# An audio tower on one core: sparsemax refinement over eight rows at once, and expert gathers one expert further ahead

## Chip, core and metric

The kernel runs on one core of a Trainium2 chip. The metric is the device time of one launch in microseconds (us), smaller is better. It was run three times, and one further execution was recorded by the hardware profiler.

## What is computed

The reference has three parts, cut here to what matters:

```python
h = tokens(x)                                  # patches of 200 samples, rfft, |.| and angle, 202->808 gelu ->128
# attention with sparsemax, 16 sequences of 256 tokens, 8 heads of 64
sim  = einsum(q, k) * 64**-0.5                 # 256x256 scores per head
attn = maximum(sim - tau, 0)                   # tau per row: the row of attn sums to 1
h = h + (attn @ v) @ W_out + b_out
# experts: each of 8 experts takes the 1024 tokens of highest probability (softmax over all 4096 tokens)
vals, idx = top_k(softmax(xn2 @ Wr, axis=0).T, 1024)
out_e = gelu(xn2[idx] @ W1 + b1) @ W2 + b2
h = h + zeros.at[idx].add(vals * out_e)
```

## The kernel before

The 4096 tokens are 32 tiles of 128, in 8 groups of 512 tokens (two sequences each). Three stages follow one another.

**Front and attention rounds.** Spectra and token features come first. Then each round handles the attention of one group, while TensorE (PE) also does the token layers and the q, k, v projections of later groups. The order on PE and ScalarE (ACT) is the list `PLAN` (L66), the order on VectorE (DVE) is `STEPS` (L85). Both are written by hand, and semaphores join them. A group's scores are four pairs `d` (0 to 3) of score tiles; a pair has two halves `u` of four rows of 128x256, so eight rows per partition. For each pair DVE takes the largest 8 of every row (`largest`, L1038), the next 8 (`thresholds` L1050, or `laced_thresholds` L1074), computes a threshold `tau` from these 16, and compares the sixteenth with `tau` (L1068, L1099). If it is above, more than 16 values may count and the threshold may need refinement. Two small reductions (L1070 and L1071) say this for each half and for both; GpSimd (POOL) takes the maximum over partitions (`anymore`, L453, L457). `settle` (L1184) reads the result into a register and branches. Where a half is marked, `surplus` (L1108) sums `max(score - tau, 0)` for its four rows (L1111) and tests whether any sum exceeds 1 by more than 3e-6; if so, `newton` (L1129) counts the values above `tau` (L1132), corrects it and calls `surplus` again. Only one half is refined at a time: half 1 if it is marked, otherwise half 0. If both are marked, L1195 puts a 2 into the test so that the rest always runs, and then `passes` (L1149, L1178) refines half 0 too. At the end L1205 writes `minus_tau`, for which ACT waits (L644, L646) before PE can transpose the result ("turn", L829).

**The choice of tokens.** This stage is serial. After the last residual (L1300), second norm (L1301, through `layernorm` L351) and logits, a softmax follows (L1312 to L1326, with eleven constants written at L1319 to L1324). Fifteen steps of `two_bits` find each expert's threshold in probability; DVE compares, PE adds up (L889). Then the tokens above the threshold are counted by themselves (L1363 to L1370, `total` at L897), and two calls of `ranks` give each chosen token its slot.

**The experts.** For expert e, `one_hots` (L1402) writes a 128x(32x128) comparison `lo_hot` and a product `hi_val`, PE multiplies them (`expert_slots`, L906), and `slots` (L1419) turns the product into row numbers and weights. POOL then issues eight indirect DMAs that gather 1024 rows (`gather`, L501), PE transposes them (`expert_columns`, L920), multiplies by W1 (`expert_hidden`, L933), ACT applies gelu, PE multiplies by W2 (`expert_out`, L947), DVE adds the bias and the weight (`weighted`, L1436), and POOL issues eight indirect DMAs that add 1024 rows to the output (`scatter`, L510). Rows, slot lists, weights and results each have two buffers. The semaphores are `slots_ok` (slots written), `xg_used` (gathered rows used), `y_ok` (half a result ready), `y_free` and `y_out` (all earlier scatters landed, L513). On POOL the order is gather 0, 1, 2, scatter 0, and then one gather and one scatter in turn; scatters 5, 6 and 7 come last, one behind the other.

Of the kernel before, what the change touches and what calls it, by code (L numbers as in the profile page):

```python
# [7 lines left out]
ds = bass.ds  # L8
# [119 lines left out]
def audio_tower(nc, x, tok_w1, tok_b1, tok_w2, tok_b2, w_qkv, w_out, b_out, w_r, e_w1, e_b1, e_w2, e_b2,  # L128
# [37 lines left out]
    with ctx:  # L166
# [3 lines left out]
        def carve(name, words):  # L170
# [3 lines left out]
            def stage(start=0):  # L174
                at = [start]

                def cut(shape, dt=f32):
# [85 lines left out]
        more = sb("more", [P, 4, 3])  # L263
        more_all = sb("more_all", [P, 4, 3], i32)
        seg16 = sb("seg16", [P, 8, 16])
        inv16 = sb("inv16", [P, 8, 16])
        r_sum = sb("r_sum", [P, 4])
        r_cnt = sb("r_cnt", [P, 4])
# [3 lines left out]
        go_5 = sb("go_5", [P, 5])  # L272
        tau_u = sb("tau_u", [P, 4])
        twice = sb("twice", [P, 1], i32)
# [70 lines left out]
                 "rest_ok", "vals_ok", "cnt_in", "rk_in", "hot_ok",  # L345
# [81 lines left out]
        def _(g):  # L427
# [73 lines left out]
            def gather(e, p):  # L501
# [3 lines left out]
                for s in range(CT):  # L505
# [30 lines left out]

        @block.scalar
        def _(a):
# [136 lines left out]
            c.up("slot0", BITS // 2 + 3)  # L675
# [23 lines left out]
        def _(t_):  # L699
# [197 lines left out]
            total(3 * BITS // 2, [gt])  # L897
            for n, m in enumerate((eq, sel)):
                t_.wait_ge(sems["rk_in"], n + 1)
                job = c.job(0)  # L900
                o = slot(job)
                mm(o[:, 0:E * NT], not_before[:, :], m[:, :, :].rearrange("p e j -> p (e j)"), start=True, stop=True)
# [3 lines left out]
            def expert_slots(e):  # L906
                t_.wait_ge(sems["hot_ok"], e + 1)
                job = c.job(3)
                o = slot(job)
                for j in range(NT):  # L910
                    last = mm(o[:, 0:5 * CT], lo_hot[:, j, :], hi_val[:, j, :, :].rearrange("p v s -> p (v s)"),
                              start=(j == 0), stop=(j == NT - 1))
                done(job, last)

            def expert_columns(n, p):
# [6 lines left out]
                return job  # L922

            def expert_hidden(n, p, ahead=None):
                t_.wait_ge(sems[f"ew_in{p}"], (n + 1) * 64)
                emptied((2, c.t["slot2"].now()))
                t_.sem_inc(sems["xg_used"], 1)
# [25 lines left out]
            expert_slots(0)  # L953
            expert_slots(1)
            expert_columns(0, 0)
            with t_.Fori(0, E // 2 - 1) as n:
                c.enter(n, 0, {"slot0": 4, "slot1": 4, "slot2": 2, "slot3": 4})
                for p in range(2):
                    hidden = expert_hidden(n, p, n * 2 + (2 + p))
                    expert_columns(n + p, 1 - p)  # L960
# [562 lines left out]
```

## Time and profile before

| | us |
|---|---|
| median of 3 runs | 903.33 |
| lowest, highest | 898.98, 903.69 |
| the profiled execution, its own time | 908.21 |
| its span, first to last instruction | 906.4 |
| busy in the span: PE, DVE, ACT, POOL | 682.0, 605.2, 456.9, 207.0 |

The profiled execution is 4.9 us (0.5%) above the median of the runs. Busy shares of the whole span say little here, since the three stages have different limits: the front and the attention rounds last until about 609 us, the choice of tokens until about 685 us, the experts until the end. Times of single instructions below are counted from the start of the span.

### The profile page before, as it was taken

How to read it: one execution, taken by the hardware profiler on the slowest of the kernel's cores; microseconds unless marked ns; L12 is line 12 of the kernel's file. 1: busy time of each engine (PE TensorE's matmuls, PEld its weight loads, DVE VectorE, ACT ScalarE, POOL GpSimd, SP SyncE). 2: the span in 40 equal slices, each digit the busy share in tenths (PEclk: the TensorE clock that was granted, in tenths of full speed). 3: DMA queues.
4: the chain of work that ended last, by engine and by line, in shares of the span. 5: the costliest groups of instructions: out<-in, count | busy, mean ns of one | idle time of the engine just before them, and what ended most of it. 6: DMA issues, size and time to landing. Idle time of an engine off the chain costs nothing. (4 is left out here: it accounts for less than half of the span.)

```text
span 906.4 us, 13135 instructions
## 1 busy us (share of the span) xinstructions
PE 682.0 (75%) x4060; PEld 449.3 (50%) x4060; DVE 605.2 (67%) x2215; ACT 456.9 (50%) x664; POOL 207.0 (23%) x212
## 2 busy tenths in 40 slices
PE   5598679679989997499999998663322996667890
PEld 3254265356565574275575765452211665544570
DVE  2868887588868868788877889846888455432110
ACT  3958638357766764478778777652000231222120
POOL 1000010001000010010010010002005588888776
PEclk9889989889999999699999998895555897779895
DMA  5200000000000000000000000005001153344333
GB/s 156 80 1 1 1 1 1 1 2 13 2 3 13 2 2 13 2 2 13 2 13 3 1 13 1 13 1 157 0 0 33 38 87 43 63 69 69 68 33 29
DMA packets 34722, 23.69 MB, mean 26 GB/s; under 512 B 8232, under 2 KB 31226, under 8 KB 34628
## 3 DMA queue, kind: packets, MB, share of 16 engines
q0 software_dynamic: 11264, 8.40, 6.9%
q1 hardware_dynamic: 23152, 14.21, 5.6%
q8 instruction: 28, 0.46, 0.2%
q14 instruction: 66, 0.54, 0.2%
q10 hardware_dynamic: 212, 0.08, 0.0%
HBM read 14.29 MB, written 8.39 MB: 25 GB/s over the span
## 5 line engine op out<-in xcount | busy, mean ns | idle before, releaser
L549 ACT ACTIVATE front<-ps 128x1024 f32<-128x1024 f32 x128 | 127.8, 1026 | 37.2 <-PE ps L796 13.3
L646 ACT ACTIVATE front<-front,minus_tau 128x256 f32<-128x256 f32 x256 | 108.6, 497 | 57.6 <-DVE minus_tau L1205 56.4
L549 ACT ACTIVATE back<-ps 128x1024 f32<-128x1024 f32 x72 | 73.7, 1024 | 82.6 <-PE ps L920 68.5
L457 POOL CROSS_LANE_REDUCE more_all<-more 128x3 int32<-128x3 f32 x32 | 15.2, 475 | 429.0 <-DVEq L1103 290.9
L829 PE MATMUL ps<-ident,front 128*128 128x128 f32 x512 | 77.0, 300 | 47.4 <-ACTq L648 22.9
L519 POOL DMA_INDIRECT out_dram<-back x64 | 102.6, 1603 | 27.4 <-issue 20.2
L549 ACT ACTIVATE back<-ps,back 128x1024 f32<-128x1024 f32 x32 | 35.4, 1114 | 130.2 <-remote 59.3
L829 PEld LDWEIGHTS ps<-ident,front 128*128 128x128 f32 x512 | 65.0, 154 | 70.2 <-issue 37.4
L947 PE MATMUL ps<-back 128*128 128x128 f32 x512 | 68.4, 300 | 22.3 <-ACT back L549 20.3
L506 POOL DMA_INDIRECT back<-rows,back x64 | 63.5, 992 | 75.6 <-issue 71.3
L947 PEld LDWEIGHTS ps<-back 128*128 128x128 f32 x512 | 66.2, 214 | 26.3 <-issue 26.3
L1077 DVE MATCH_REPLACE8 back<-top,front 128x256 f32<-128x256 f32 x176 | 69.7, 409 | 0.0
L845 PE MATMUL ps<-back,front 128*64 128x256 f32 x512 | 68.5, 396 | 1.3 <-ACT back L549 1.2
L819 PE MATMUL ps<-front 64*128 64x256 f32 x512 | 67.3, 398 | 2.0 <-issue 1.2
L933 PE MATMUL ps<-back 128*128 128x512 f32 x128 | 63.4, 637 | 6.8 <-issue 3.6
L1046 DVE MAX8 top<-front 128x8 f32<-128x256 f32 x168 | 58.7, 413 | 10.0 <-issue 5.9
L1080 DVE MAX8 top<-back 128x8 f32<-128x256 f32 x176 | 59.7, 411 | 1.6
L796 PE MATMUL ps<-xcur,wqkv 128*128 128x512 f32 x128 | 58.7, 611 | 2.0 <-ACT front L572 1.3
L819 PEld LDWEIGHTS ps<-front 64*128 64x128 f32 x512 | 47.5, 191 | 16.5 <-issue 10.2
L751 PE MATMUL ps<-back,w1m 101*128 101x512 f32 x96 | 52.7, 632 | 2.3 <-issue 2.3
L769 PE MATMUL ps<-w2t,hid 128*128 128x128 f32 x384 | 46.9, 284 | 9.1 <-ACT hid_r L607 7.6
L450 POOL TENSOR_TENSOR rstd<-var_eps,minus_half 128x4 f32<-128x4 f32 x16 | 19.5, 1219 | 145.5 <-DVE var_eps L360 145.5
(191 smaller groups left out, 1092.8 us busy)
## 6 DMA issues: line engine op xcount, KB each, us to landing
back<-in_L_ffn_W_dram SPq DMA_DIRECT2D x16, 256.0 KB
front<-in_x_dram SPq DMA_DIRECT2D x4, 750.0 KB, 4.5
rows<-xn SPq DMA_DIRECT2D x8, 256.0 KB, 2.2
out_dram<-h SPq DMA_DIRECT2D x1, 2048.0 KB, 7.8
back<-rows,back POOLq DMA_INDIRECT x64
out_dram<-back POOLq DMA_INDIRECT x64
wqkv<-in_L_attn_W_qkv_dram SPq DMA_DIRECT2D x1, 768.0 KB, 6.0
back<-in_L_ffn_b_dram SPq DMA_DIRECT2D x8, 64.0 KB
```

What stands on the lines that cost most here:

```text
L506: g.indirect_dma_start(xg[p][:, s, :], None, rows2[:, :], bass.IndirectOffsetOnAxis(ap=gather_at[p][:, s:s + 1], axis=0))\
L519: g.indirect_dma_start(orow[:, :], bass.IndirectOffsetOnAxis(ap=add_at[p][:, s:s + 1], axis=0), y[p][:, s, :], None, compute_op=ALU.add)\
L549: a.activation(dst, ps[s][:, 0:cols], func, **kw).then_inc(sems[f"free{s}"], 1)
L646: a.activation(prob[n % 2][:, r, :], sc[n][:, r, :], ACT.Relu, bias=minus_tau[:, n // 2, n % 2 * 4 + r:n % 2 * 4 + r + 1])
L796: last = mm(o[:, q * 512:(q + 1) * 512], wqkv[:, m * P:(m + 1) * P], xcur[:, :], start=True, stop=True)
L819: last = mm(o[:, a_ * 512 + it * SEQ:a_ * 512 + (it + 1) * SEQ], z[r, hp, b * SEQ + it * P:b * SEQ + (it + 1) * P], z[r, 4 + hp, b * SEQ:( ...
L829: last = nc.tensor.transpose(o[:, a_ * 512 + jb * SEQ + it * P:a_ * 512 + jb * SEQ + (it + 1) * P], prob[n % 2][:, 2 * a_ + it, jb * P:(jb ...
L845: last = mm(o[a_ * DH:(a_ + 1) * DH, hp * SEQ:(hp + 1) * SEQ], v_sb[p][:, 2 * b + jb, hd * DH:(hd + 1) * DH], prob_t[n % 2][:, 2 * a_ + jb ...
L933: last = mm(o[:, q * 512:(q + 1) * 512], ew1[p][:, m * P:(m + 1) * P], xg_t[:, q * 512:(q + 1) * 512], start=True, stop=True)
L947: last = mm(o[:, s * D:(s + 1) * D], eh[:, k, s * P:(s + 1) * P], ew2[p][:, k, :], start=(k == 0), stop=(k == F // P - 1))
L1077: v.match_replace(sc2[:, r, :], top[d % 2][:, r, 0:8], sc[2 * d + r // 4][:, r % 4, :], LOWEST)
L1080: last = v.max(top[d % 2][:, r, 8:16], sc2[:, r, :])
```

## The change

**Refinement.** The two reductions of a marked pair become one number: the comparison itself sums its outcome over the eight rows (`accum_out`), and POOL reduces one column instead of three. `surplus` and `newton` take all eight rows of the pair, with their row numbers known at compile time, and write `tau` in place. The copies into `tau_u`, the forced test, `twice` and `passes` are gone.

**The choice of tokens.** The statistics of two of the last group's four tiles are taken before the last residual; eleven constants are written while the logits are on their way; the count of tokens above the threshold is in the same PE job as the first `ranks`.

**Experts.** In `one_hots(0)` and `one_hots(1)` the large comparison comes last and in four quarters, each with a semaphore, so that PE can begin. In `slots` the row numbers are written directly as integers and released at once; the weights follow. Experts' slots are computed one expert further ahead. POOL issues gathers 0 to 3, then scatter 0, gather 4, and so on; the last gather is split in two halves, before and after scatter 4. On PE, the slots of expert e+4 stand between the transposes of expert e+2 and the second product of expert e+1.

```diff
@@ thresholds and laced_thresholds
-                v.tensor_tensor(above[:, :], top[d % 2][:, :, 15], tau[:, d, :], ALU.is_gt)
-                v.drain()
-                v.tensor_reduce(more[:, d, 0:2], above[:, :].rearrange("p (u r) -> p u r", r=4), AX.X, ALU.max)
-                v.tensor_reduce(more[:, d, 2:3], above[:, :], AX.X, ALU.max)
+                v.scalar_tensor_tensor(above[:, :], top[d % 2][:, :, 15], 1.0, tau[:, d, :], ALU.mult, ALU.is_gt,
+                                       accum_out=more[:, d, :])
@@ surplus, newton
-            def surplus(d, u):
+            def surplus(d):
-                for r in range(4):
-                    v.scalar_tensor_tensor(sc2[:, r, :], half(d, u, r), tau_u[:, r:r + 1],
+                for r in range(8):
+                    v.scalar_tensor_tensor(sc2[:, r, :], sc[2 * d + r // 4][:, r % 4, :], tau[:, d, r:r + 1],
...
-            def newton(d, u):
+            def newton(d):
-                for r in range(4):
-                    v.tensor_scalar(sc2[:, 4 + r, :], half(d, u, r), tau_u[:, r:r + 1], None, ALU.is_gt, ALU.add,
-                                    accum_out=r_cnt[:, r:r + 1])
+                for r in range(8):
+                    v.tensor_scalar(sc2[:, r, :], sc[2 * d + r // 4][:, r % 4, :], tau[:, d, r:r + 1], None,
+                                    ALU.is_gt, ALU.add, accum_out=r_cnt[:, r:r + 1])
...
@@ settle
-                    v.tensor_tensor(go_5[0:1, 4:5], more_all[0:1, d, 0:1], more_all[0:1, d, 1:2], ALU.add)
-                    u = v.value_load(more_all[0:1, d, 1:2], min_val=0, max_val=1)
-                    v.tensor_copy(tau_u[:, :], tau[:, d, ds(u * 4, 4)])
-                    v.drain()
-                    surplus(d, u)
+                    surplus(d)
@@ POOL
-            gather(0, 0)
-            gather(1, 1)
-            gather(2, 0)
+            for e in range(4):
+                gather(e, e % 2)
             scatter(0, 0, first=True)
-            with g.Fori(0, (E - 4) // 2) as n:
-                for p in range(2):
-                    gather(n * 2 + (3 + p), 1 - p)
-                    scatter(n * 2 + (1 + p), 1 - p)
-            gather(E - 1, 1)
-            scatter(E - 3, 1)
-            scatter(E - 2, 0)
-            scatter(E - 1, 1)
+            gather(4, 0)
+            with g.Fori(0, (E - 6) // 2) as n:
+                for p in (1, 0):
+                    scatter(n * 2 + (2 - p), p)
+                    gather(n * 2 + (6 - p), p)
+            scatter(E - 5, 1)
+            gather(E - 1, 1, range(CT // 2))
+            scatter(E - 4, 0)
+            gather(E - 1, 1, range(CT // 2, CT))
+            for e in range(E - 3, E):
+                scatter(e, e % 2)
@@ PE, experts
-            expert_slots(0)
-            expert_slots(1)
+            expert_slots(0, quarters=0)
+            expert_slots(1, quarters=4)
             expert_columns(0, 0)
...
+            columns_used()
+            hidden = expert_hidden(0, 0, 2)
+            expert_columns(0, 1)
+            expert_slots(3)
+            columns_used()
+            expert_out(0, hidden)
+            with t_.Fori(0, (E - 4) // 2) as n:
...
+                for p in (1, 0):
+                    hidden = expert_hidden(n + (1 - p), p)
+                    expert_columns(n + 1, 1 - p)
+                    expert_slots(n * 2 + (5 - p))
+                    columns_used()
                     expert_out(p, hidden)
@@ DVE, slots
+                v.scalar_tensor_tensor(gather_at[p][:, :], parts[:, 0, :], float(P), parts[:, 1, :], ALU.mult, ALU.add)
+                v.drain().then_inc(sems["slots_ok"], 1)
@@ DVE, experts
             one_hots(0, first=True)
+            slots(0, 0, first=True)
+            one_hots(1, quarters=True)
+            slots(0, 1, first=True)
+            for p in range(2):
+                one_hots(2 + p)
+                slots(1, p)
+            weighted(0, 0)
+            with v.Fori(0, (E - 4) // 2) as n:
                 c.enter(n, 0, {"slot3": 4})
                 for p in range(2):
+                    one_hots(n * 2 + (4 + p))
+                    slots(n + 2, p)
+                    weighted(n + p, 1 - p)
+                c.leave((E - 4) // 2)
+            for e in range(E - 3, E):
+                weighted(e // 2, e % 2)
```

## Rows read from the trace of the kernel before

**Rows 1.** Busy time by stretch: span, PE, PEld, DVE, ACT, POOL, clock, DMA, GB/s.
```profile
400.00:500.00 100.00, 99.76 (x606) 64.40 (x605) 79.16 (x321) 75.20 (x116) 7.93 (x11) 1.00 0.02 7
800.00:850.00 50.00, 34.86 (x204) 26.67 (x203) 13.58 (x55) 8.30 (x8) 40.29 (x32) 0.83 0.37 55
```

**Rows 2.** Waits: engine, line, releaser: total us, times, longest.
```profile
ACT front L646 <- DVE minus_tau L1205: 56.4, 8, 20.4
```

**Rows 3.** Timeline of DVE, the last marked pair: start, us, line.
```profile
351.38 0.13 DVE L1195 TENSOR_TENSOR go<-more_all 1x1 f32<-1x1 int32 x1
...
352.68 0.48 DVE L1111 SCALAR_TENSOR_TENSOR back<-front,tau_u,zero 128x256 f32<-128x256 f32 x1 [0.20 <-issue]
...
357.82 0.06 DVE L1165 MEMSET go<- 1x1 f32 x1 [1.53 <-issue]
...
366.99 0.17 DVE L1152 COPY tau_u<-tau 128x4 f32<-128x4 f32 x1 [0.86 <-issue]
...
372.27 0.17 DVE L1205 TENSOR_SCALAR minus_tau<-tau 128x8 f32<-128x8 f32 x1 [1.43 <-issue]
```

**Rows 4.** Timeline, PE, the first work behind that pair.
```profile
375.52 1.94 PE L829 MATMUL ps<-ident,front 128*128 128x128 f32 x8 [18.33 <-ACT front L549]
```

**Rows 5.** Groups of DVE instructions: busy us, mean ns, idle before.
```profile
L1111 DVE SCALAR_TENSOR_TENSOR back<-front,tau_u,zero 128x256 f32<-128x256 f32 x32 | 13.6, 481 | 1.2 <-issue 1.0
L1132 DVE TENSOR_SCALAR_CACHE_REDUCE back<-front,tau_u 128x256 f32 x8 | 3.4, 476 | 0.2
L1070 DVE TENSOR_REDUCE more<-above 128x2 f32<-128x8 f32 x10 | 1.6, 163 | 0.7
```

**Rows 6.** Timeline of DVE, first marked pair and second marked pair.
```profile
170.18 0.06 DVE L1165 MEMSET go<- 1x1 f32 x1 [4.17 <-issue]
...
190.73 0.13 DVE L1195 TENSOR_TENSOR go<-more_all 1x1 f32<-1x1 int32 x1
...
196.66 0.17 DVE L1205 TENSOR_SCALAR minus_tau<-tau 128x8 f32<-128x8 f32 x1 [1.37 <-issue]
```

**Rows 7.** Timeline of DVE, the choice of tokens.
```profile
609.87 0.87 DVE L355 BATCH_NORM_STATS2 stats<-h 128x6 f32<-128x128 f32 x4
...
620.65 0.20 DVE L1318 RECIPROCAL all_sum<-all_sum 128x8 f32<-128x8 f32 x1 [0.54 <-POOL all_sum L485]
...
621.97 0.43 DVE L1326 TENSOR_TENSOR front<-front,all_sum 128x256 f32<-128x256 f32 x1
...
669.34 0.69 DVE L1376 TENSOR_TENSOR_SCAN front<-front,ps 128x256 f32<-128x256 f32 x1 [0.73 <-PE ps L903]
```

**Rows 8.** Timeline, the first expert's one-hots, slots and gather.
```profile
675.78 4.42 DVE L1408 TENSOR_TENSOR front<-front 128x4096 bf16<-128x4096 bf16 x1
...
683.48 0.20 DVE L1423 COPY front<-ps 128x40 f32<-128x40 f32 x1 [1.37 <-PE ps L911]
...
685.47 1.31 POOL L506 DMA_INDIRECT back<-rows,back  x1 [52.43 <-issue]
```

**Rows 9.** Timeline of POOL, gathers (L506) and scatters (L519).
```profile
690.86 2.01 POOL L506 DMA_INDIRECT back<-rows,back  x1 [0.30 <-issue]
...
711.24 0.95 POOL L506 DMA_INDIRECT back<-rows,back  x1 [4.28 <-DVEq L1434]
...
725.36 1.64 POOL L519 DMA_INDIRECT out_dram<-back  x1 [3.76 <-DVEq L1460]
...
741.31 1.02 POOL L506 DMA_INDIRECT back<-rows,back  x1 [0.30 <-issue]
...
751.42 1.62 POOL L519 DMA_INDIRECT out_dram<-back  x1 [0.30 <-issue]
...
870.54 1.55 POOL L519 DMA_INDIRECT out_dram<-back  x1 [2.56 <-DMA out_dram<-back]
```

**Rows 10.** Timeline of DVE, slots of expert 2 and the one-hots behind them.
```profile
709.20 0.20 DVE L1423 COPY front<-ps 128x40 f32<-128x40 f32 x1 [6.79 <-PE ps L911]
...
716.79 1.49 DVE L1415 TENSOR_TENSOR front<-front 128x1280 bf16<-128x1280 f32 x1 [0.19 <-issue]
```

More of the change, by code:

```diff
@@ L499, in _, with gather @@
             orow = out.rearrange("b s d -> (b s) d")
-            def gather(e, p):
+            def gather(e, p, half=range(CT)):
                 g.wait_ge(sems["slots_ok"], e + 1)
@@ L504, in gather @@
                 g.sem_inc(sems["pool_held"], 1)
-                for s in range(CT):
+                for s in half:
                     g.indirect_dma_start(xg[p][:, s, :], None, rows2[:, :],
@@ L901, in _ @@
                 o = slot(job)
+                if m is eq:
+                    rows = o[:, E * NT:E * (NT + JB)].rearrange("p (r j) -> p r j", j=JB)
+                    for j in range(0, NT, JB):
+                        mm(rows, ones[:, :], gt[:, :, j:j + JB], start=(j == 0), stop=(j + JB == NT))
                 mm(o[:, 0:E * NT], not_before[:, :], m[:, :, :].rearrange("p e j -> p (e j)"), start=True, stop=True)
@@ L904, in _, with expert_slots @@
                              start=True, stop=True))
[L906 to L907 removed]
+            def expert_slots(e, quarters=None):
+                if quarters is None:
+                    t_.wait_ge(sems["hot_ok"], e + 1)
                 job = c.job(3)
@@ L1171, in rest_of_refinement @@
                             with v.If(go_on()):
-                                newton(d, u)
+                                newton(d)
                             v.drain()
                         v.drain()
-                v.tensor_copy(tau[:, d, ds(u * 4, 4)], tau_u[:, :])
-                v.tensor_tensor(twice[0:1, :], more_all[0:1, d, 0:1], more_all[0:1, d, 1:2], ALU.mult)
-                v.drain()
-                with v.If(v.value_load(twice[0:1, 0:1], min_val=0, max_val=1) > 0):
-                    passes(d, 0)
                 v.drain()
@@ L1400, in _, with compared, one_hots @@
             v.sem_inc(sems["held"], 1)
-            def one_hots(e, first=False):
+            def compared(j0, j1):
+                for j in range(j0, j1):
+                    v.tensor_scalar(lo_hot[:, j, :], iota_b[:, :], lo_e[:, j:j + 1], None, ALU.is_equal)
+            def one_hots(e, first=False, quarters=False):
                 v.tensor_copy(lo_e[:, :], lo_f[:, ds(e, 1), :].rearrange("p e j -> p (e j)"))
@@ L1406, in one_hots @@
                 va = vals[:, ds(e, 1), :, :].rearrange("p e j n -> p (e j) n")
-                if first:
-                    v.tensor_tensor(lo_hot[:, :, :], iota_b[:, :].unsqueeze(1).to_broadcast([P, NT, P]),
-                                    lo_e[:, :].unsqueeze(2).to_broadcast([P, NT, P]), ALU.is_equal)
-                for j in range(0 if first else NT):
-                    v.tensor_scalar(lo_hot[:, j, :], iota_b[:, :], lo_e[:, j:j + 1], None, ALU.is_equal)
+                if not first and not quarters:
+                    compared(0, NT)
                 v.tensor_tensor(hi_hot[:, :, :], iota_r[:, 1:CT + 1].unsqueeze(1).to_broadcast([P, NT, CT]),
@@ L1416, in one_hots @@
                                 va.unsqueeze(3).to_broadcast([P, NT, 5, CT]), ALU.mult)
+                for q in range(4 if quarters else 0):
+                    compared(q * NT // 4, (q + 1) * NT // 4)
+                    v.drain().then_inc(sems["hot_quarter"], 1)
+                for q in range(4 if first else 0):
+                    rows = slice(q * NT // 4, (q + 1) * NT // 4)
+                    v.tensor_tensor(lo_hot[:, rows, :], iota_b[:, :].unsqueeze(1).to_broadcast([P, NT // 4, P]),
+                                    lo_e[:, rows].unsqueeze(2).to_broadcast([P, NT // 4, P]), ALU.is_equal)
+                    v.drain().then_inc(sems["hot_quarter"], 1)
                 v.drain().then_inc(sems["hot_ok"], 1)
```

149 lines of the change are left out of this document (67 added, 82 removed).

## The prediction

> **What bounds the kernel now.** I read the busy time by stretch first, then the waits of each stretch, then timelines around the places that the diff touches. In the middle of the attention rounds PE is busy all the time at full clock, DVE 79% [rows 1]: there an instruction less on DVE is worth nothing. The exceptions are pairs that need refinement. ACT waited eight times for `minus_tau`, 56.4 us in all, 20.4 once [rows 2]. In the expert stage POOL is busy 81% of a stretch, the rest being 0.30 us gaps between its DMA instructions [rows 1, 9], while PE, ACT and DVE wait for it. So there the time is POOL's first gather, plus its fixed work, plus its waits. Between the two lies the serial choice of tokens, where each saved link of the chain counts in full.
>
> **Refinement.** 32 sums and 8 counts [rows 5] are 8 calls of `surplus` and 2 of `newton`, at four rows each. One `surplus` belongs to `passes` [rows 3] and two to `newton`, so five pairs were marked. The last is the dear one: from L1195 to `minus_tau` 351.38 to 372.27, that is 20.9 us, with PE idle for 18.3 us [rows 3, 4]. `passes` ran, so both its halves were marked, and then the code forces a `newton` whether it is needed or not. The trace can't say whether it was; the inputs can. In the reference's scores exactly one row of all has more than 16 counted values (18, first group, last pair). Four other pairs have rows with just 16, in the last of them one in each half, and in these the threshold is already right: the largest sum exceeds 1 by 1.9e-6, under the limit of 3e-6. I take it that this last pair needs no `newton`.
>
> Price of one call after the change. A simple refinement before (second marked pair) took 190.73 to 196.66, 5.9 us [rows 6]. Before its first sum stand 1.3 us that mostly go (L1195, a register load, a copy; 351.38 to 352.68 in [rows 3]); I leave 0.2. Sums follow each other at 0.41 us (481 ns with overlap, rows 5), so eight take 3.3 us where four took 1.7. The test behind and the branch stay, 3.3 us. Together 6.8 us: **+0.9 us for each of three simple pairs**. The last pair, simple now: 6.8 against 20.9, **-14.0 us**. The first pair does need `newton`: +0.9, then four more counts (+1.6, 476 ns each overlapped, rows 5), four more sums (+1.6), and the copy, the product and the test for `passes` go (-1.9, an estimate from the idle time around such branches of 0.9 to 1.5 us, rows 3): **+2.2 us**. The 4.17 us of idle time before its first `newton` [rows 6] I keep; it was 1.53 us the second time [rows 3], so with other code it may be 2.6 lower or as much higher. Sum: 3 x 0.9 + 2.2 - 14.0 = -9.1 us.
>
> Thresholds: a comparison, a drain and two small reductions (163 ns, rows 5) become one operation with an accumulator read, which the trace has for L1111 at 81 ns; about 0.23 us less in each of 32 pairs, 7 us of DVE. Hidden where PE is full. It counts only where DVE sets the pace (ahead of the four smaller stalls and in the last round): a third, **-2.5 us**; bounds 0 and -7. POOL's reduction of one column instead of three lies beside DVE's work: nothing. What is late next: with `minus_tau` at 358.3, PE, out of work since 357.2 [rows 4], still waits about 4 us. It then runs L829 in 1.94 us at the low level (half of 2.4 GHz) as after 18 us; regaining clock would be a gain of 0 to 2 us, I take 0. Attention: -9.1 - 2.5 = **-11.6 us**.
>
> **Choice of tokens.** Two of four tile statistics leave the path: 0.87 us becomes about 0.5, the aggregation likewise: -0.5. The constants between the reciprocal's end (620.85) and L1326 (621.97) [rows 7] move under the wait for the logits: -1.0. The separate count goes, its four matmuls and its reduction stay: -0.5 (DVE waited 0.73 us for L903, rows 7; bounds 0 and -1.6). `one_hots(0)`: the comparison of 4.42 us [rows 8] becomes four of about 1.2 with drains (+0.5), but PE's 32 matmuls, between it and L1423, run beside it except the last eight: net -0.35 (bounds +0.5, -0.9). From L1423 to the gather 2.0 us passed (683.48 to 685.47, rows 8); three small operations, of the kind of 163 ns in [rows 5], and the gaps between them now come after the release: -0.45. Together **-2.8 us**: POOL's first gather starts at 682.7 instead of 685.5 [rows 8].
>
> **Experts.** POOL's fixed work doesn't change: 64 gathers, 64 scatters, eight gathers in 10.1 us (741.31 to 751.42, rows 9). Only its waits do. Before: 4.3 us for the slots of expert 2 and 3.8 us for the first result, the usual gap of 0.3 included [rows 9]. After: gather 1 ends 2.8 us earlier, at 704.2 (before, the wait for gather 2 began at 711.24 - 4.28 = 706.96). Expert 2's slots depend on PE, which began with the first gather's rows: L1423 at 706.4 instead of 709.2 [rows 10]. From there to the gather 2.0 us passed; with the earlier release 1.4. Gather 2 starts at 707.8 and, by the step from 711.24 to scatter 0 less its wait, POOL is free again at 718.4. From L1423 to the end of the next one-hots 9.1 us pass (709.20 to 716.79 + 1.49, rows 10), so expert 3's are done at 715.5; L1423 follows 1.4 us behind [rows 8], at 716.9, and gather 3 may start at 718.3. That just meets gather 2's end, so gather 3 runs without a wait, to 728.5. Scatter 0's first half was ready at 725.4 [rows 9]; its product now stands behind the slots on PE, at most 3 us later, and is hidden still. Before, scatter 0 began at 725.36 with gather 3 still to come, which makes 735.5. Hence **-7.0 us** in all, of it 2.8 from the earlier start. What queues behind gather 3's wait is scatter 0 and everything after it; a late slot costs its lateness one to one. Later each slot list and each `y_free` comes in time, since POOL takes 26 us for an expert (725.36 to 751.42, rows 9) and PE, busy 70% [rows 1], 18. The split of the last gather leaves 5 us between scatters 3, 4 and 5; a landing cost 2.56 us where nothing stood between (870.54, rows 9), so no new wait. SP's weights hang on `ew_used`, early in both.
>
> On POOL's DMA instructions one finds 2.01 us instead of 0.95 at 690.86 [rows 9], beside L1415 on DVE; the 32 comparisons of L1411 leave them at 0.95. The Trainium skill (page SBUF — State Buffer, section "SBUF: two separate sides") says that descriptors for DMAs issued by GpSimd can't be written while a two-port DVE operation runs, some 3100 ns instead of 620. Here only the first of these two rows looks like it.
>
> **Sum.** -11.6 - 7.0 = -18.6 us, 889.6 for the profiled execution (908.21). That one lay 4.9 us above the median, so against 903.33 the forecast is **884.7 us**.
>
> **Rivals.**
> 1. *The last marked pair still iterates.* The trace showed one `newton` there. If the chip's rounding puts one of its sums above the limit, then `newton` and a second `surplus` follow: 1.5 idle, 3.3 counts, 1.2 small ones, 3.3 sums, 1.9 test: 11.2 us of the 14 are lost. For it: the trace can't exclude it. Against: the margin by the inputs, and the three other pairs with 16 values passed. 896 us. Chance 0.07.
> 2. *POOL's front stalls again.* Gather 3 waits for the slots of expert 3 (a tie above) as long as gather 2 did: 4 us, 889 us. Chance 0.11. Or the gather that now falls beside DVE's work lengthens: 1.06 us for each DMA that falls as at 690.86 [rows 9], 8.5 us for its eight, 893 us. Against: comparisons all along the first gathers left the others at 0.95. Chance 0.04. (This is the skill's rule on the shared port, named above, as it would act here.)
> 3. *The stall at the last pair moves on.* PE gets `minus_tau` 14 us earlier, but DVE, busy 80% [rows 1], is then what the next turns wait for, and half returns: 892 us. Against: DVE keeps its distance to PE, as both move. Chance 0.08.
> 4. *Slower: refinement does not end.* All eight rows must now meet the limit. A row whose sum is stuck above 1 + 3e-6 by rounding of `tau` would run `newton` up to 26 times at 11.2 us, 290 us for one pair. From the second superfluous `newton` on (22 us) the change is a loss. Place: any of five pairs. Against: the step of `tau` near 2.4 times 16 values is under the limit, and unmarked rows by the inputs stay under 2.9e-6. Two superfluous ones give 907 us, a stuck row about 1170. Chance 0.04.
>
> The forecast keeps 0.66; its own spread is 879 to 890 (thresholds 0 to -7, code loading 2.6 either way, clock up to 2, token stage 1). The range that holds the time 8 times in 10 takes in rivals 2 and 3: 876 to 893. A run of this kernel can tell about 0.5% from no change, so faster is below 898.8: forecast and rivals 1 to 3, **0.94**; same 0.02; slower 0.04.
>
> **What would show it.** `surplus` 5 calls plus 1, so 48 sums and 8 counts; no second `newton`; PE's idle time before L829 near 350 about 4 us; `minus_tau` 6.8 us after each marked pair begins. POOL: first gather about 14 us earlier than 685.5, about 46 us from it to scatter 0 (39.9 before, with a gather less), no wait above 1 us until the last two scatters. Wrong would be: a second `newton` anywhere but the first pair, a wait at gather 3, or PE idle behind the shortened stall.

## The result and the profile after

| | before | after |
|---|---|---|
| median, us | 901.15 (4 runs) | 872.8 (4 runs, 867.34 to 873.6) |
| the profiled execution | 908.21 | 873.6 |
| its span | 906.4 | 871.7 |
| busy: PE, DVE, ACT, POOL | 682.0, 605.2, 456.9, 207.0 | 675.0, 598.2, 456.4, 201.8 |

The ratio is 0.9672, 95% interval [0.9619, 0.9724]: faster, 28.4 us by the medians. Forecast were 18.6 us, 884.7 and a range of 876 to 893. The sign was right, the size wrong, and the range missed the time. One execution of 3654.64 us, in the second run of the attention part alone (experiment 6), is in none of the ratios.

Between three landmarks the profiles say where it went. The reciprocal root for the last norm, POOL's last work of the attention part, starts at 586.55 instead of 611.53: 25.0 us. POOL's first gather starts at 657.29 instead of 685.47, 3.2 us more. From there to the start of the last scatter instruction pass 208.0 us (to 865.27) instead of 215.2 (to 900.62), 7.2 us more.

The refinement of the last marked pair, timeline of DVE after (start, us, line; answers to [rows 3]):

```profile
341.15 0.14 DVE L1114 SCALAR_TENSOR_TENSOR above<-top,tau 128x8 f32<-128x8 f32 x1
...
342.93 0.46 DVE L1121 SCALAR_TENSOR_TENSOR back<-front,tau,zero 128x256 f32<-128x256 f32 x1
...
346.32 0.16 DVE L1125 TENSOR_REDUCE go_w<-r_sum 128x1 f32<-128x8 f32 x1
...
348.02 0.14 DVE L1136 TENSOR_SCALAR go<-go_s 1x1 int32<-1x1 f32 x1
349.55 0.17 DVE L1191 TENSOR_SCALAR minus_tau<-tau 128x8 f32<-128x8 f32 x1 [1.39 <-issue]
```

One test, no count behind it: 6.6 us from the first of the eight sums to `minus_tau`. PE's timeline there, its wait for ACT, and the groups of sums and counts (answer to [rows 4, 2, 5]):

```profile
352.80 1.06 PE L829 MATMUL ps<-ident,front 128*128 128x128 f32 x8 [1.98 <-ACT front L549]
```

```profile
ACT front L646 <- DVE minus_tau L1191: 36.5, 6, 12.5
```

```profile
L1121 DVE SCALAR_TENSOR_TENSOR back<-front,tau,zero 128x256 f32<-128x256 f32 x48 | 20.0, 480 | 0.9 <-issue 0.8
L1142 DVE TENSOR_SCALAR_CACHE_REDUCE back<-front,tau 128x256 f32<-128x256 f32 x8 | 3.3, 476 | 0.9 <-issue 0.9
```

48 sums and 8 counts are as forecast: six calls of `surplus`, one `newton`, at the first pair. PE now idles 2 us instead of 18.3, and the same eight transposes take 1.06 us, not 1.94: it came back at the full clock. By stretch (span, PE, PEld, DVE, ACT, POOL, clock, DMA, GB/s), first before, then after:

```profile
270.00:280.00 10.00, 7.07 (x22) 4.28 (x23) 8.69 (x35) 4.30 (x6) 2.48 (x2) 0.83 0.09 29
340.00:400.00 60.00, 41.43 (x234) 25.59 (x233) 49.57 (x216) 32.17 (x54) 1.28 (x3) 0.83 0.02 6
```

```profile
270.00:280.00 10.00, 10.00 (x43) 5.44 (x41) 9.59 (x41) 8.09 (x12) 1.01 (x1) 1.00 0.10 29
340.00:400.00 60.00, 57.78 (x358) 37.41 (x354) 51.24 (x212) 44.07 (x71) 3.72 (x6) 1.00 0.02 6
```

Tokens and the first gather, timelines of DVE and POOL after (answer to [rows 7, 8]):

```profile
585.42 0.49 DVE L1296 BATCH_NORM_STATS2 stats<-h 128x6 f32<-128x128 f32 x2
...
595.66 0.20 DVE L1331 RECIPROCAL all_sum<-all_sum 128x8 f32<-128x8 f32 x1 [0.54 <-POOL all_sum L483]
595.94 0.42 DVE L1333 TENSOR_TENSOR front<-front,all_sum 128x256 f32<-128x256 f32 x1
...
649.93 5.25 DVE L1429 TENSOR_TENSOR front<-front 128x1024 bf16<-128x1024 bf16 x4
655.76 0.20 DVE L1438 COPY front<-ps 128x40 f32<-128x40 f32 x1 [0.57 <-PE ps L917]
```

```profile
657.29 1.47 POOL L504 DMA_INDIRECT back<-rows,back  x1 [48.58 <-issue]
...
680.08 0.94 POOL L504 DMA_INDIRECT back<-rows,back  x1 [2.17 <-DVEq L1443]
...
686.35 1.89 POOL L504 DMA_INDIRECT back<-rows,back  x1 [0.30 <-issue]
...
701.03 1.64 POOL L517 DMA_INDIRECT out_dram<-back  x1 [0.30 <-issue]
```

POOL waits once, 2.17 us, in front of gather 2; gather 3 and scatter 0 (701.03) follow without a wait. Before, there were 4.28 and 3.76 us [rows 9]. Behind them the longest wait in either profile is some 2.5 us, ahead of the last two scatters.

### The profile page after: what moved, and what is told of

It reads as the page before. It is cut to its first block and busy times, and to the rows that moved or that the text cites. A ratio compares the mean times of both kernels' runs of the same rounds, so it can differ in the third digit from the quotient of the medians.

```text
span 871.7 us, 12946 instructions
## 1 busy us (share of the span) xinstructions
PE 675.0 (77%) x4060; PEld 447.2 (51%) x4060; DVE 598.2 (69%) x2170; ACT 456.4 (52%) x664; POOL 201.8 (23%) x212
## 5 line engine op out<-in xcount | busy, mean ns | idle before, releaser
L517 POOL DMA_INDIRECT out_dram<-back x64 | 100.5, 1570 | 23.8 <-issue 22.6
L455 POOL CROSS_LANE_REDUCE more_all<-more 128x1 int32<-128x1 f32 x32 | 11.5, 358 | 398.4 <-DVEq L1116 265.3
L829 PE MATMUL ps<-ident,front 128*128 128x128 f32 x512 | 75.0, 295 | 30.0 <-ACTq L648 21.6
L829 PEld LDWEIGHTS ps<-ident,front 128*128 128x128 f32 x512 | 63.3, 151 | 52.6 <-ACTq L648 31.7
L845 PE MATMUL ps<-back,front 128*64 128x256 f32 x512 | 70.8, 408 | 1.2 <-ACT back L549 1.2
L940 PE MATMUL ps<-back 128*128 128x512 f32 x128 | 58.4, 609 | 1.4 <-ACT back L549 1.4
```

The lines of the kernel that those rows point to most:

```text
L517: g.indirect_dma_start(orow[:, :], bass.IndirectOffsetOnAxis(ap=add_at[p][:, s:s + 1], axis=0), y[p][:, s, :], None, compute_op=ALU.add)\
L829: last = nc.tensor.transpose(o[:, a_ * 512 + jb * SEQ + it * P:a_ * 512 + jb * SEQ + (it + 1) * P], prob[n % 2][:, 2 * a_ + it, jb * P:(jb ...
L845: last = mm(o[a_ * DH:(a_ + 1) * DH, hp * SEQ:(hp + 1) * SEQ], v_sb[p][:, 2 * b + jb, hd * DH:(hd + 1) * DH], prob_t[n % 2][:, 2 * a_ + jb ...
L940: last = mm(o[:, q * 512:(q + 1) * 512], ew1[p][:, m * P:(m + 1) * P], xg_t[:, q * 512:(q + 1) * 512], start=True, stop=True)
```

## The experiments

Every ratio is to the kernel before, run on the same chip. In the expectations, theory A is my reading of the two profiles unless they say otherwise.

**1. The attention part alone**, all of the diff's refinement and threshold hunks and nothing else.

```diff
-            def surplus(d, u):
+            def surplus(d):
...
-            def newton(d, u):
+            def newton(d):
...
-                v.tensor_reduce(more[:, d, 2:3], above[:, :], AX.X, ALU.max)
```

> The kernel before with the refinement and threshold part of the change alone. Theory A (the surplus over the forecast lies in the attention rounds: the shorter stall at the last marked pair also gives PE's clock back, and a threshold is worth 0.40 us, not 0.23): 24 to 26 us less than before, 876 us, a ratio of 0.972; POOL's L450 for the last norm near 587 instead of 611.5. Theory B (the forecast of this part was right and something outside it gave the rest): 11.6 us less, 889 us, 0.987.

Ratio 0.9759 [0.9729, 0.9789], 22.9 us by the medians. Its 32 threshold marks on POOL come within 0.4 us of after's, and the power of the last norm starts at 587.06, 24.5 us earlier: the attention gain is this part's. That the time fell by less is a matter of the experts' stage on this chip (experiment 6).

**2. Only the forced pass taken away** from the kernel before.

```diff
-                    v.tensor_tensor(go_5[0:1, 4:5], more_all[0:1, d, 0:1], more_all[0:1, d, 1:2], ALU.add)
+                    v.memset(go_5[0:1, 4:5], 0.0)
```

> The kernel before, but a pair with both halves marked no longer forces a newton (a zero stands where the sum of the two marks stood), so half 0 of such a pair is left unrefined. Theory A: minus_tau of the last marked pair comes 15 us sooner, PE waits 2 to 3 us instead of 18.3 and keeps its clock: 16.5 to 18 us less in all, 884 us, 0.981. Rival, as in the forecast (no clock regained): 14 us less or under, 887 to 890 us. Second rival: a newton runs all the same, since a sum really exceeds the limit on the chip: under 3 us less.

0.9903 [0.9869, 0.9937], 9.1 us by the medians, far less than expected. The pair itself gave what it should: the next mark comes at 368.84 instead of 381.15, 12.3 us. It left an idle stretch of DVE in front of `minus_tau` (3.64 us, where the changed kernel has 1.39), and PE, idle 5.7 us, still came back at the low clock (1.94 us for eight transposes):

```profile
359.96 0.17 DVE L1205 TENSOR_SCALAR minus_tau<-tau 128x8 f32<-128x8 f32 x1 [3.64 <-issue]
```

```profile
363.21 1.94 PE L829 MATMUL ps<-ident,front 128*128 128x128 f32 x8 [5.69 <-ACT front L549]
```

At the last norm 9.4 us are left, against 25.0 for the whole attention part. Alone, then, the forced pass is worth less than half of it. The changed kernel gets more out of the same pair, 14.3 us from mark to `minus_tau`, and keeps PE's clock behind it.

**3. The old marks back** in the changed kernel.

```diff
-                v.scalar_tensor_tensor(above[:, :], top[d % 2][:, :, 15], 1.0, tau[:, d, :], ALU.mult, ALU.is_gt,
-                                       accum_out=more[:, d, :])
+                v.tensor_tensor(above[:, :], top[d % 2][:, :, 15], tau[:, d, :], ALU.is_gt)
+                v.drain()
+                v.tensor_reduce(more[:, d, 0:2], above[:, :].rearrange("p (u r) -> p u r", r=4), AX.X, ALU.max)
+                v.tensor_reduce(more[:, d, 2:3], above[:, :], AX.X, ALU.max)
```

> The changed kernel with the old mark of a threshold (comparison, drain, two reductions, three columns reduced on POOL). The forecast charged the mark at 0.23 us each and a third of them on the path: 2.5 us more than after. The traces of before and after show the mark some 0.40 to 0.42 us shorter at each step that DVE paces, but from step 18 on TensorE holds the end of most rounds: by that, 32 marks x 0.41 = 13 us if all counted, 4 to 7 us more than after as I take it. No difference at all would say that the whole of the attention gain is the pairs' refinement.

0.9781 [0.9745, 0.9817], against 0.9657 for the changed kernel itself on that chip: 9.2 us by the medians, more than the 4 to 7 expected. The last mark comes 8.7 us later, the last norm 6.3 us later (592.98 instead of 586.68), and the wait in front of the third gather is 1.5 us longer. Not all of it is the marks themselves. With them PE waits 4.30 us behind the last marked pair instead of 1.76 and comes back at the low clock, and an idle stretch of DVE that is not in the changed kernel, 2.51 us at 467.11, shows that the code behind them has moved (experiment 4). But the small term of my sum was a large one. The timelines of a mark show why, before and after:

```profile
248.19 0.15 DVE L1099 TENSOR_TENSOR above<-top,tau 128x8 f32<-128x8 f32 x1
248.42 0.16 DVE L1101 TENSOR_REDUCE more<-above 128x2 f32<-128x8 f32 x1
248.49 0.15 DVE L1102 TENSOR_REDUCE more<-above 128x1 f32<-128x8 f32 x1
248.95 0.43 DVE L1046 MAX8 top<-front 128x8 f32<-128x256 f32 x1 [0.30 <-issue]
```

```profile
244.44 0.14 DVE L1114 SCALAR_TENSOR_TENSOR above<-top,tau 128x8 f32<-128x8 f32 x1
244.51 0.08 DVE L1114 DVE_READ_ACCUMULATOR above<-top,tau 128x1 f32 x1
244.89 1.41 DVE L1063 MAX8 top<-front 128x8 f32<-128x256 f32 x4 [0.30 <-issue]
```

From the comparison to the next MAX8 it is 0.45 us instead of 0.76, and POOL's reduction, for which `minus_tau` waits, is shorter by 0.12 us (475 to 358 ns in the mean of 32). Together some 0.4: on POOL's timeline 18 of the 31 steps from one mark to the next are 0.36 to 0.46 us shorter. Nine of them lie ahead of 410 in the kernel before (3.8 us in all) and five behind 540 (2.0 us). The four between are returned at the next round's first mark: after leads by 24.9 us at 425, 483 and 540 alike. So the traces of before and after, without any experiment, show 5.8 us of marks on the path.

**4. Code that never runs.** Two more calls of `newton` inside the innermost branch of every pair, or 32 more in the first pair alone, or one copy fewer in every pair. The diffs stand in this order. In all three DVE executes the same instructions as in the changed kernel.

```diff
                             with v.If(go_on()):
                                 newton(d)
+                                newton(d)
+                                newton(d)
```

```diff
                             with v.If(go_on()):
                                 newton(d)
+                                for _ in range(32 if settled.now() == 1 else 0):
+                                    newton(d)
```

```diff
                 newton(d)
                 with v.If(go_on()):
-                    newton(d)
-                    with v.If(go_on()):
-                        with v.Fori(0, 24):
+                    with v.Fori(0, 24):
...
```

> The changed kernel with two more passes of the refinement written inside the innermost branch, which the data never enters: DVE's program grows from 4505 to 5945 instructions, and no instruction more is executed. Theory I (the two idle stretches of 2.3 and 2.5 us on DVE in front of minus_tau that vanished with the change were DVE waiting for its own program): 2 to 6 us more than after, such stretches are back. Theory R (what counts are the instructions executed): within 0.7 us of after, no such stretch over 1.5 us.

> The changed kernel with the refinement's rest written shorter: after the first newton the loop of up to 24 passes follows at once, without a second copy of newton ahead of it (one pass fewer in the worst case; the data needs one). DVE's program shrinks from 4505 instructions to about 3800, nothing executed changes. Theory D (DVE's idle stretches come from the length of code that each branch jumps over): the stretches before minus_tau shrink, 1 to 5 us less than after. Theory P (they come from where in the program a pair's code lies, not from the length): any sign, up to 3 us either way, and the stretches sit at other pairs. Theory R (code that is not executed costs nothing): within 0.7 us of after.

> The changed kernel with 32 more passes of newton (720 instructions) written into the never entered loop of the first pair alone, so that all code of the other 31 pairs lies further back and is unaltered in itself. Theory D: at most one stretch more, at the first pair, of 1 to 3 us, which TensorE hides there; time within 1 us of after. Theory P: stretches of 1.5 to 2.5 us come and go at other pairs as with the longer program, 2 to 6 us more (or less) than after.

Longer: 0.9718 [0.9688, 0.9748], 5.0 us slower than the changed kernel beside it. Shorter: 0.9678 [0.963, 0.9726], not faster. Shifted: 0.9645 [0.9601, 0.9688], no difference. So the length that a branch jumps over does not decide (theory D falls), and unexecuted code is not free (R falls): what remains is where a pair's code lies. Theory P is borne out by the stretches, which come and go at other pairs, but not by the time of the shifted program, which moved by less than it said.

Against after, with executed work unchanged, the times of POOL's marks move in single jumps. Those above 2 us are -2.4, +2.3, +2.2 and +2.7 near 188, 235, 358 and 400 in the longer program, -2.3, +2.2, +2.9, +2.4 and -2.5 near 188, 342, 400, 468 and 515 in the shorter one, +2.2 and -2.2 near 235 and 283 in the shifted one. Most other steps agree within 0.05 us. Where the marks come later, except near 400, an idle stretch of DVE stands in front of `minus_tau` (shorter, then shifted code); near 188 and 283 one of after's own is gone (2.57 us at 176.59, 2.51 at 262.81):

```profile
464.44 0.17 DVE L1189 TENSOR_SCALAR minus_tau<-tau 128x8 f32<-128x8 f32 x1 [2.47 <-issue]
```

```profile
228.07 0.17 DVE L1193 TENSOR_SCALAR minus_tau<-tau 128x8 f32<-128x8 f32 x1 [2.25 <-issue]
```

and in the kernel before, whose two at 229.48 and 486.57 are gone after:

```profile
229.48 0.17 DVE L1205 TENSOR_SCALAR minus_tau<-tau 128x8 f32<-128x8 f32 x1 [2.34 <-issue]
486.57 0.17 DVE L1205 TENSOR_SCALAR minus_tau<-tau 128x8 f32<-128x8 f32 x1 [2.46 <-issue]
```

The jumps near 400 are another thing: there DVE waits for ACT, and PE had run 350 to 360 at 0.70 of its clock in the longer program and 0.66 in the shorter one, against 1.00 in after. In both a stretch in front of a marked pair's `minus_tau` (3.57 us at 352.07, 3.70 at 320.15, where after has 1.39 and 1.17) had delayed the work; PE waited 3.9 and 3.4 us behind the last marked pair instead of 2.0 and came back at the low clock. Longer program, PE and DVE:

```profile
355.31 1.94 PE L829 MATMUL ps<-ident,front 128*128 128x128 f32 x8 [3.89 <-ACT front L549]
```

```profile
384.64 0.87 DVE L353 BATCH_NORM_STATS2 stats<-emb 128x6 f32<-128x128 f32 x4 [2.83 <-ACT emb L612]
```

The DMA view has a queue that carries instructions (packets, MB, share). In 227 to 230 of before, and in 462 to 465 of the shorter program, it moves one packet just as DVE stands still:

```profile
q14 instruction: 1, 0.01, 0.8%
```

```profile
q14 instruction: 1, 0.01, 1.1%
```

Such packets pass all the time, so two examples prove little. In the profiles of before, after, experiment 3 and these three programs, 15 of DVE's 18 idle stretches of 2.2 us and more by "issue", between 150 and 610 us, hold one. Of the 168 windows of 2.4 us in front of a `minus_tau` without such a stretch, 16 do.

The Trainium skill (page Runtime: NRT & Kernel Launch, section "Instruction fetch mechanics") says that instructions are prefetched in order, in blocks of 16 KiB, and that a taken branch to a target outside the two blocks at hand has to wait for a DMA. By that rule the waits would follow position, as they do here, and cost 2.2 to 2.4 us each by the marks; how much of the program is at hand no run shows. That DVE waits for its code in these stretches is the reading that fits the positions and the packets; no row names it.

Some jumps are given back where PE holds the round, as the -2.5 near 515. The shorter program's last norm starts at 586.83, 0.3 us from after's, though its last mark is 2.8 us behind: from there to the norm PE's clock made it 13.7 us against after's 16.2. Nor are the longer program's 5.0 us all stretches. By the marks 2.7 of them are the jump near 400, and 1.3 lie between the first and the third gather. In front of the third, all three programs and experiment 3 wait 3.1 to 3.4 us instead of 1.7 to 2.2: from 17.5 to 20 us behind the first gather PE ran at 0.74 to 0.84 of its clock in the changed kernel's three profiles and at 0.50 in these four.

**5. Experts and tokens alone**, all other hunks on the kernel before, and the changed kernel with the old order of gathers.

```diff
-            for e in range(4):
-                gather(e, e % 2)
+            gather(0, 0)
+            gather(1, 1)
+            gather(2, 0)
             scatter(0, 0, first=True)
```

> The kernel before with everything else of the change (choice of tokens, one-hots, slots, order of gathers). Theory A: 10.4 us less (3.2 in the choice of tokens, 7.2 in the experts), 891 us, 0.988, and nothing moves ahead of the last residual. Theory B: 17 us less or more, 884 us, 0.981. If the two parts do not add up to 28 us, they depend on each other.

> The changed kernel with POOL's order of before: three gathers, scatter 0, then gather and scatter in turn, the last gather in one piece. Theory A: POOL stands idle between gather 2 (ends 690.7) and scatter 0, whose first half is ready near 696.6, so 5.5 to 6.5 us more than the changed kernel, 879 us, ratio to before 0.974. Rival (gathers in front only trade places with scatters, the gain came from earlier slots): 1 us more or under, 0.968.

The first gave 1.0004 [0.9978, 1.003]: nothing. The second gave 0.9787 [0.9736, 0.9838], some 10 us over the changed kernel's ratio. In both profiles DVE, doing nothing else, took several experts' slots 2.1 to 3.3 us after PE's last matmul for them. Experts and tokens alone, timelines of PE and DVE, and of POOL, which waits for it:

```profile
691.02 0.45 PE L919 MATMUL ps<-front 128*128 128x40 bf16 x8 [1.11 <-issue]
694.50 0.20 DVE L1471 COPY front<-ps 128x40 f32<-128x40 f32 x1 [3.57 <-remote]
```

```profile
695.83 0.95 POOL L506 DMA_INDIRECT back<-rows,back  x1 [2.81 <-DVEq L1476]
708.78 0.95 POOL L506 DMA_INDIRECT back<-rows,back  x1 [2.33 <-DVEq L1476]
721.70 0.94 POOL L506 DMA_INDIRECT back<-rows,back  x1 [2.25 <-DVEq L1476]
```

The same kind of row is in the profile of before on which I had predicted: the matmuls end at 771.6, the copy starts at 779.68.

```profile
770.64 0.97 PE L911 MATMUL ps<-front 128*128 128x40 bf16 x32
...
779.68 0.20 DVE L1423 COPY front<-ps 128x40 f32<-128x40 f32 x1 [10.59 <-remote]
```

**6. Kernel or chip?** The changed kernel again, on a second chip; then, on a third, before, experts and tokens alone, three gathers, and the changed kernel once more.

> The changed kernel, unaltered, as a control on the chip of this batch. Theory A (the expert part is worth what the profile of after shows, wherever it runs): ratio to before 0.965 to 0.969, the slots' copies come 0.6 to 1.4 us behind the start of their last matmul group, POOL waits only once, some 2.2 us, in front of the third gather. Theory B (the parts run before in this study, which showed slots' copies 2 to 4 us late in front of gathers on another chip or in other runs, show a state of the chip or of the run and not of the code): the control shows them too, and a ratio of 0.970 to 0.975.

> The kernel before, unaltered. In its first profile DVE's copies of an expert's slots start 6 to 9 us behind the matmuls that fill them, in 4 of 8 experts, while neither DVE nor TensorE is busy. Theory S (such late starts come and go with the chip or the run): where the other kernels of this batch show none, this one shows none, and first gather to last scatter is under 213 us instead of 215.2. Theory K (they belong to the kernel's order of work): they are there as before, whatever the others show, and the stretch is 215 to 216 us.

> The expert and token part of the change alone, a second time. On the first chip it gave a ratio of 1.000, with slots' copies 2 to 3 us late in front of the second, third and fourth gather. Theory S: on this chip the copies come as in the profiles of after, POOL waits only once for some 2 us, and the ratio is 0.988 to 0.992 (7 us from first gather to last scatter and 3 us ahead of it). Theory K: the late copies are there again, and the ratio is 0.997 to 1.003.

> The changed kernel with three gathers in front of the first scatter, a second time. The code up to the third gather is that of after. On the first chip its slots' copies were 3 us late and the time 10 us over after's. Theory S: no late copies here, and 5 to 7 us more than after. Theory K: late copies again in front of the second gather, and 9 to 11 us more than after.

> The changed kernel, unaltered, for the other three of this batch: median 869 to 875 by both theories, 1.7 to 2.2 us of wait in front of the third gather. If e2_again and e6_again show late copies and this one does not, they belong to the kernels; if all show them, to the chip.

| | ratio | first gather to last scatter, us |
|---|---|---|
| after, second chip | 0.9657 [0.9632, 0.9682] | 207.8 |
| before, third chip | 1.0 [0.9982, 1.0019] | 211.5 |
| experts and tokens alone, third chip | 0.9949 [0.9929, 0.9969] | 208.8 |
| three gathers, third chip | 0.9723 [0.9683, 0.9763] | 215.0 |
| after, third chip | 0.965 [0.9605, 0.9695] | 207.8 |

On these chips no kernel shows a late copy; in before it starts 0.04 us behind the end of the matmuls (756.19 plus 0.97, then 757.20):

```profile
757.20 0.20 DVE L1423 COPY front<-ps 128x40 f32<-128x40 f32 x1 [2.56 <-PE ps L911]
```

The same two kernels give 1.0004 on one chip and 0.9949 on another. Theory S holds: the late copies are a state of the chip or the run. The profile of before had been taken in it; the profile of after shows none. Without late copies, POOL's waits at the front of before are 3.30 us in all instead of 8, and the expert order is worth 3.7 us (211.5 to 207.8), not 7.2. What makes the copies late is open: the trace names no instruction of the core as their releaser, and no run tells more. The fourth gather is worth 5.4 us by the medians of the third chip (875.45 to 870.07): with the new order on PE and DVE but the old one on POOL, scatter 0 waits.

```profile
689.71 1.64 POOL L517 DMA_INDIRECT out_dram<-back  x1 [6.50 <-DVEq L1473]
```

The two belong together: half of the expert change alone is worse than none of it (215.0 against 211.5).

> The refinement and threshold part alone, a second time, to see whether the parts add up on a chip without late slots' copies (the first time they were there, and the ratio 0.976). Sum of parts: after 0.9657, experts and tokens alone 0.9949 on such a chip, so attention alone 0.970 to 0.973; the last norm's power at 587 less what the start of the run differs by.

The attention part alone now gives 0.9699 [0.965, 0.9747]. With 0.9949 for the rest that makes 0.965, the ratio of the whole: the parts add up.

**7. A faster version.** The slots of expert 2 computed after the first hidden group instead of the second, and the quarters of the first one-hots signalled by the comparison, without a drain.

```diff
-                    if m == 1 and ahead is not None:
+                    if m == 0 and ahead is not None:
...
-                    v.drain().then_inc(sems["hot_quarter"], 1)
+                        .then_inc(sems["hot_quarter"], 1)
```

> The changed kernel with the slots of the expert ahead computed behind the first of four hidden groups instead of the second, and the quarters of the first one-hots signalled by the comparison itself instead of a drain. If the one wait that POOL has left in front of its third gather (2.2 us) ends with that expert's slots, and POOL bounds the stage: 2.0 to 2.7 us less than after. If POOL's wait only moves to another place: within 0.7 us of after.

> The shorter refinement code together with the sooner slots, as the version that might beat both kernels: their two differences from after added up, 1.5 us for the slots by the trace (pow to last scatter) and whatever the shorter code gives, so ratio to before about 0.958 to 0.964; no wait over 0.3 us on POOL between its first gather and scatter 6.

0.9629 [0.9603, 0.9654], the best ratio measured, 4.2 us below the changed kernel on that chip, though the intervals overlap ([0.9632, 0.9682]). POOL's last wait at the front is gone. Only 1.5 us of it are the edit's by the trace (from the last norm to the last scatter, 277.4 us instead of 278.9); the profiled run had also come to the first mark 4.3 us earlier, where no code differs. Together with the shorter refinement: 0.9667 [0.9628, 0.9707] instead of the 0.958 to 0.964 expected. POOL's waits are gone as expected, but the shorter code's jumps are in it too.

## Why the prediction was wrong

The step that failed is the attention part: 11.6 us forecast (12.1 with the statistics ahead of the last norm), 25.0 measured at that norm. In it, the thresholds were mis-sized and the clock was put at nothing.

- **Refinement, forecast -9.1.** Right in mechanism, slightly small. From POOL's mark to `minus_tau` the five pairs went from 20.4, 7.3, 9.6, 7.0 and 22.3 us to 21.1, 7.9, 10.0, 7.5 and 8.1: +0.7, +0.6, +0.3, +0.5 and -14.3, -12.2 in all. The last pair was -14.0 in the forecast and needs no `newton`, as the inputs had said: rivals 1 and 4 are out. The first pair was too dear at +2.2, and the simple ones at +0.9, since more of L1195's and the copy's overhead went.
- **Thresholds, forecast -2.5: this step failed.** It took 0.23 us per mark and a third of the marks. It is some 0.4 at more than half of them: 5.8 us on the path by the traces of before and after, while experiment 3 measures 6.3 us at the last norm and 9.2 in time, with clock and moved code in it. I had summed durations and left out the drain's gap, and had put POOL's shorter reduction down as hidden ("lies beside DVE's work: nothing") although `minus_tau` waits for it. I had also read the 99.8% of PE's busy time in 400 to 500 [rows 1] as "worth nothing there". It is so in the middle rounds, and POOL's marks show it: near 457 they lead by 27.5 us and at the next round's first mark by 24.9 again. But up to 400 the rounds follow DVE.
- **Clock, forecast 0: this failed too.** Taken at the low end of 0 to 2, for a PE that would still wait about 4 us; it waited 1.98. In all nine profiles in which PE waited 1.7 to 2.0 us there, the eight transposes took 1.06 or 1.07 us, in all nine in which it waited 3.4 us or more, 1.94. What the low clock costs at the next round's first mark is the jump near 400 of experiment 4, 2.7 to 2.9 us (in experiment 3 it is 1.9 with a mark of 0.4 in it). PE's stretch 340 to 400 rose from 0.83 to 1.00, and so did 270 to 280; L829 behind the last pair gained 0.9 us of 1.94. Part was given back at the end, where after ran at 0.67 in 560 to 570 (0.83 in the shifted program, whose last norm starts 2.4 us earlier): from last mark to last norm after needs 16.2 us, before 14.3.
- **Loading of code, forecast 0 with 2.6 either way.** The size of one stretch was right; I had allowed for one place only, the first `newton`. Two of 2.3 and 2.5 us vanished elsewhere; the second, at 486.57, was returned at the next round's first mark. At the last mark after leads by 26.9 us. Refinement and marks make 12.2 + 5.8 = 18.0 of it. An estimate from the rows above adds 2.7 for the clock behind the last pair and 2.3 for the stretch at 229.48; the other 3.9 stay open, and no run changes one of these alone. The 1.9 us given back behind the last mark leave the 25.0.
- **Tokens, forecast -2.8.** Measured 0.5 ahead of the last norm and 3.2 behind it. Constants -1.0 (the gap between reciprocal and product fell from 1.32 to 0.28), release of the slots -0.45 (1.99 to 1.53) as forecast. The quarters gave nothing: 5.25 us for four against 4.42 for one, 7.99 us from first one-hots operation to copy instead of 7.96. What is left for the count is 1.7 instead of 0.5, at its bound of 1.6.
- **Experts, forecast -4.2 behind the first gather.** Profile to profile it was 7.2, because gather 2 waited 2.17 us where I had it wait 3.6, and 0.9 us went behind scatter 0. But before had been profiled with late copies; without them the step is 3.7 us, near the 4.2 forecast. That is partly luck: of the two waits that I priced, 4.3 and 3.8 us, only one of 3.3 is left without late copies. Rival 2's wait at gather 3 did not come, nor did a row of lengthened gathers: single ones of 1.25 and 1.89 us stand among the first 32, as at 690.86 before [rows 9]. So the rule that the prediction weighed from the Trainium skill (page SBUF — State Buffer, section "SBUF: two separate sides") shows in at most one gather at a time here, if it is that rule: whether the operation beside such a gather, the TENSOR_TENSOR of L1415 at 690.86 before, is a two-port one, no run tells.
- **Rival 3** (half of the pair's gain returns) is out: POOL's marks keep 23.0 us of lead behind the last pair, against 8.5 ahead of it.

## What to carry over

Where DVE sets the pace, price a small step by the distance between the starts of its neighbours, and follow its result through every engine to the one who waits. Busy shares decide what is hidden only for their own stretch, so a term that recurs 32 times deserves a look at each recurrence. Before a wait in a profile becomes a term of the sum, ask whether its executions always have it: a copy that starts long after its releaser has ended is a sign of a disturbed one.

## What the runs showed of the hardware

- Code that is never executed shifted the time by 5.0 us (0.9718 against 0.9657): through idle stretches of DVE, which made marks 2.2 to 2.4 us later (15 of 18 stretches hold a packet of the instruction queue), and through PE's clock behind them.
- Behind one and the same place, the wait for the last marked pair, PE came back at full clock after 1.7 to 2.0 us without work (nine profiles, eight transposes in 1.06 or 1.07 us) and at the low one after 3.4 to 18.3 us (nine profiles, 1.94 us). The low clock made the next round's first mark 2.7 to 2.9 us later.
- From the last mark to the last norm the 18 profiles need either 13.7 to 14.3 us (eleven) or 16.0 to 16.7 us (seven), at granted clocks that differ. The attention part alone shows both: 16.7 us with 0.67 in 560 to 570, 14.2 us with 0.83. A comparison at the last norm is no better than these 2.4 us.
- On one chip, in each of four kernels, DVE took several experts' slots 2.1 to 10.4 us behind the end of the matmuls it had waited for; in twelve profiles on two other chips never.
- Two profiled executions of the kernel before reach the first threshold mark at 100.72 and at 94.28 us. From the fifteenth mark on they stay 5.0 to 5.2 us apart. Such a head start is no part of a change's worth, which is why the experiments are compared from landmark to landmark.
